# Cross-attention's output chain moved to other slots, context rounding split, weight loads of the feed-forward stage moved

## What is computed

```
x = layernorm(x + self_attention(x))         # LoRA linears, 16 heads of 32
x = layernorm(x + cross_attention(x, ctx))   # 16 heads of 16 channels
x = layernorm(x + ffn(x))                    # fp8 rounding, gelu gate, hidden 2048
```

## Time and profile before

| | us |
|---|---|
| median of 3 runs | 1977.44 |
| lowest and highest | 1976.67, 1979.93 |
| profiled execution, its own time | 1983.12 |
| its span, first to last instruction | 1981.2 |
| busy in the span: PE, DVE, ACT, POOL | 1900.6, 1495.3, 1124.2, 981.4 |
| mean granted TensorE clock | 0.972 |

### The profile page before, as it was taken

One profiled execution on the slowest core, in us unless ns is written; L12 is line 12 of the kernel. 1 busy time (PEld: TensorE's weight loads), 2 busy tenths in 40 slices (PEclk: granted clock), 3 DMA queues, 4 the chain that ended last, 5 costly groups with the idle time before them and its releaser, 6 DMA issues.

```text
span 1981.2 us, 31819 instructions
## 1 busy us (share of the span) xinstructions
PE 1900.6 (96%) x11460; PEld 1056.7 (53%) x11460; DVE 1495.3 (75%) x2632; ACT 1124.2 (57%) x2117; POOL 981.4 (50%) x968
## 2 busy tenths in 40 slices
PE   7999999999999898999999999999999899999997
PEld 4677777777777544444444444444444334444443
DVE  3566666666675667788888888888888439999997
ACT  3345444444444526888888888888887653333330
POOL 3455546555465423444444445445443237666664
PEclk9999999999999869999999999999999879999999
DMA  5665565655646521334443333334343300111111
GB/s 169 173 165 142 145 166 134 158 140 141 171 117 165 141 78 40 120 111 125 138 141 112 106 108 107 111 104 119 119 120 118 131 28 12 44 43 43 65 43 43
DMA packets 149899, 220.56 MB, mean 111 GB/s; under 512 B 41847, under 2 KB 50551, under 8 KB 148999
## 3 DMA queue, kind: packets, MB, share of 16 engines
q1 hardware_dynamic: 140078, 216.96, 38.0%
q10 hardware_dynamic: 9664, 1.58, 0.5%
HBM read 83.95 MB, written 32.02 MB: 59 GB/s over the span
## 4 chain that ended last, share of the span: by engine, by line
PE 65%; DVE 14%; DMA 7%; POOL 6%; issue 3%; SPq 2%; ACT 2%; ACTq 0%; DVEq 0%; POOLq 0%
PE bank L1287 9%; PE bank L1322 9%; PE bank L1616 8%; PE bank L85 7%; PE bank L86 6%; PE bank L87 6%; PE bank L1330 5%; PE bank L1592 5%; PE bank L577 4%; DMA xa_den<-inv 3%; PE bank L631 2%; DVE sa_mneg L703 2%; PE bank L644 2%; DVE sa_xnat L717 2%; DVE xa_mneg L1365 2%
## 5 line engine op out<-in xcount | busy, mean ns | idle before, releaser
L1365 DVE TENSOR_REDUCE xa_mneg<-bank 128x1 f32<-128x512 f32 x1024 | 643.7, 683 | 134.3 <-PE bank L1330 132.5
L1186 ACT ACTIVATE xa_prob<-bank 128x512 f32<-128x512 f32 x1024 | 549.0, 605 | 88.0 <-PE bank L1322 84.8
L1330 PE MATMUL bank<-xa_kst,xa_qst 48*128 48x512 f32 x1024 | 386.0, 462 | 14.5 <-DMA xa_kst<-xa_part_k 8.9
L1322 PE MATMUL bank<-xa_qst,xa_kst 49*128 49x512 f32 x1024 | 367.4, 447 | 15.5 <-ACT xa_prob L1186 15.2
L468 ACT ACTIVATE sa_prob<-bank 128x512 f32<-128x512 f32 x256 | 152.2, 598 | 333.7 <-PE bank L631 332.9
L1322 PEld LDWEIGHTS bank<-xa_qst,xa_kst 49*128 49x128 f32 x1024 | 167.5, 188 | 305.1 <-ACT xa_prob L1186 248.1
L1287 PE MATMUL bank<-xa_prob,xa_v 128*32 128x512 f32 x2048 | 280.0, 619 | 0.0
L1524 POOL TENSOR_TENSOR ff_total<-ff_prod,ff_mag 128x512 f32<-128x512 bf16 x128 | 194.3, 1518 | 96.7 <-DVE ff_mag L1640 96.7
L1330 PEld LDWEIGHTS bank<-xa_kst,xa_qst 48*128 48x128 f32 x1024 | 165.4, 188 | 55.5 <-DVE xa_mneg L1365 37.4
L703 DVE TENSOR_REDUCE sa_mneg<-bank 128x2 f32<-128x512 f32 x256 | 164.1, 682 | 35.1 <-PE bank L644 34.9
L1568 ACT ACTIVATE ff_gelu<-bank 128x512 bf16<-128x512 f32 x128 | 75.7, 593 | 156.7 <-PE bank L1616 156.7
(11 more groups left out here) (191 smaller groups left out, 3626.9 us busy)
## 6 DMA issues: line engine op xcount, KB each, us to landing
xa_qst<-xa_part_q SPq DMA_DIRECT2D x192, 128.0 KB, 3.5
xa_kst<-xa_part_k SPq DMA_DIRECT2D x192, 128.0 KB, 2.8
sa_qst<-sa_part_qh SPq DMA_DIRECT2D x64, 256.0 KB, 4.1
sa_kst<-sa_part_kh SPq DMA_DIRECT2D x64, 256.0 KB, 5.4
xa_den<-inv SPq DMA_DIRECT2D x64, 256.0 KB
sa_xraw<-xT SPq DMA_DIRECT2D x32, 256.0 KB, 4.3
sa_qst<-sa_part_ql SPq DMA_DIRECT2D x32, 256.0 KB, 4.0
sa_kst<-sa_part_kl SPq DMA_DIRECT2D x32, 256.0 KB, 5.8
```

Source lines behind the costliest of these rows:

```text
L1186: act.activation(prob[place[e]][:, :], banks[eb[e]][:, :], ACT.Exp, scale=X_SCALE)\
L1322: pe.matmul(banks[eb[e]][:, :], kst[u % 3][rows_of, head // 2, t * P:(t + 1) * P], qst[u % 3][rows_of, head // 2, :], start=True, stop=Tru ...
L1330: pe.matmul(banks[mb[m]][:, :], qst[u % 3][rows_of, n // 8, t * P:(t + 1) * P], kst[u % 3][rows_of, n // 8, :], start=True, stop=True).the ...
L1365: dve.tensor_reduce(mneg[:, u % 2, column:column + 1], banks[mb[m]][:, :], AX.X, ALU.max, negate=True).then_inc(s_mfree, 1)
```

## The change

- Output chain, first half: reciprocal at 5 (was 8), write of `inv` at 6 (was 9), spread read of `den` at 10 (was 13), product on POOL at 14 (was 17).
- Output chain, second half: reciprocal and write stay at 8 and 9; `den` at 12 (was 13), product at 16 (was 17). The sum of the halves at 33 (was 34).
- The context load moves from 64b-28 to 64b-27, which puts it behind the second half's `den` on SP.
- The rounding of x and context is two instructions each (one per half of the channels), at 64b-14 and -11 for x, and 64b and +5 for the context; the low parts follow one slot later each. Semaphore counts follow.
- `bn_stats` and `bn_aggr` move three slots behind the residual addition, the factor on POOL from 2 to 5 slots behind it.
- The feed-forward phase's first step moves from slot 1022 to 1032. The two x2 loads of its second step move to its fifth (slot 1086, was 1046).
- `down` waits for `hq` piece by piece and no longer for all 16 at once.

```
     LAST = BATCH * (NB + 1) + 40
+    HIGH_AT = {"x": (-14, -11), "c": (0, 5)}
...
     def output_half(slot, after):
-        halves, left = divmod(slot - OUT_AT - after, S // 2)
-        return divmod(halves, 2) if left == 0 and 0 <= halves < 2 * U else None
+        for half, slots in enumerate(after if isinstance(after, tuple) else (after, after)):
+            u, left = divmod(slot - OUT_AT - half * S // 2 - slots, S)
+            if left == 0 and 0 <= u < U:
+                return u, half
+        return None
...
-    def high_x(act, wait, b):
+    def high_x(act, wait, b, i):
...
-        act.activation(xh[:, :, :], x1[b % 4][:, :, :], ACT.Copy).then_inc(s_hi, 1)
+        act.activation(xh[:, i, :], x1[b % 4][:, i, :], ACT.Copy).then_inc(s_hi, 1)
...
-            if (un := output_half(slot, 9)):
+            if (un := output_half(slot, (6, 9))):
...
-            if (un := output_half(slot, 13)):
+            if (un := output_half(slot, (10, 12))):
...
-            if (b := batch(slot, -28)):
+            if (b := batch(slot, -27)):
                 load_c(sp, wait, b)
...
-            if (un := output_half(slot, 17)):
+            if (un := output_half(slot, (14, 16))):
...
-            if (un := unit(slot, OUT_AT + 34, 1)):
+            if (un := unit(slot, OUT_AT + 33, 1)):
...
-            if (b := batch(slot, -13)):
-                low_x(pool, wait, b)
-            if (b := batch(slot, 1)):
-                low_c(pool, wait, b)
-            for job in jobs_in.get(slot - 2, []):
+            for i in range(CC):
+                if (b := batch(slot, HIGH_AT["x"][i] + 1)):
+                    low_x(pool, wait, b, i)
+                if (b := batch(slot, HIGH_AT["c"][i] + 1)):
+                    low_c(pool, wait, b, i)
+            for job in jobs_in.get(slot - 5, []):
...
-                    wait.wait_ge(s_pjfree, n + 1)
-                    dve.bn_stats(stats[:, t, :], x[:, t, :]).then_inc(s_bn, 1)
+            for job in jobs_in.get(slot - 3, []):
+                if job[0] == "o":
+                    _, b, t = job
+                    wait.wait_ge(s_pjfree, at[job] + 1)
+                    dve.bn_stats(stats[:, t, :], x1[b % 4][:, t, :]).then_inc(s_bn, 1)
...
-            if (un := output_half(slot, 8)):
+            if (un := output_half(slot, (5, 8))):
...
-        yield
+        for _ in range(4):
+            yield
         left.stacks(wait, 2)
         load(1)
         load(2)
-        for _ in range(PRELUDE - 2 + 2 * HT):
+        for _ in range(PRELUDE - 5 + 2 * HT):
             yield
...
             n = 4 * p + t
             wait.wait_ge(s_wo, 16)
-            wait.wait_ge(s_hq, HT * (p + 1))
             wait.wait_ge(s_sum, n - 1)
...
             for h in range(HT):
+                wait.wait_ge(s_hq, HT * p + h + 1)
                 last = pe.matmul(lb[n % 2][:, :], hq[p % 2][:, h, t * P:(t + 1) * P],
                                  wo[:, h, :], start=(h == 0), stop=(h == HT - 1))
...
-FFN_AT = [1022, 1046, 1070, 1078, 1086, 1094, 1108]
+FFN_AT = [1032, 1046, 1070, 1078, 1086, 1094, 1108]
```

More of the change, by code:

```diff
@@ L960, in load_c @@
     def load_c(sp, wait, b):
-        wait.wait_ge(s_hi, 2 * b)
-        wait.wait_ge(s_low, 2 * b)
+        wait.wait_ge(s_hi, 4 * b)
+        wait.wait_ge(s_low, 4 * b)
         sp.dma_start(craw[:, :, :], rows(a["c"], b)).then_inc(s_c, 16)
-    def high_x(act, wait, b):
+    def high_x(act, wait, b, i):
         wait.wait_ge(s_x1[b % 4], 16 * (b // 4 + 1))
@@ L968, in high_x, with high_c @@
             wait.wait_ge(s_pj, at["q", 2 * b - 1] + 1)
-        act.activation(xh[:, :, :], x1[b % 4][:, :, :], ACT.Copy).then_inc(s_hi, 1)
-    def high_c(act, wait, b):
+        act.activation(xh[:, i, :], x1[b % 4][:, i, :], ACT.Copy).then_inc(s_hi, 1)
+    def high_c(act, wait, b, i):
         wait.wait_ge(s_c, 16 * (b + 1))
@@ L974, in high_c, with low_x, low_c @@
             wait.wait_ge(s_pj, at["v", b - 1, 1] + 1)
[L975 to L979, removed]
+        act.activation(ch[:, i, :], craw[:, i, :], ACT.Copy).then_inc(s_hi, 1)
+    def low_x(engine, wait, b, i):
+        wait.wait_ge(s_hi, 4 * b + i + 1)
+        engine.tensor_tensor(xl[:, i, :], x1[b % 4][:, i, :], xh[:, i, :].bitcast(F32),
                              ALU.subtract).then_inc(s_low, 1)
-    def low_c(engine, wait, b):
-        wait.wait_ge(s_hi, 2 * b + 2)
-        engine.tensor_tensor(cl[:, :, :], craw[:, :, :], ch[:, :, :].bitcast(F32),
+    def low_c(engine, wait, b, i):
+        wait.wait_ge(s_hi, 4 * b + 2 + i + 1)
+        engine.tensor_tensor(cl[:, i, :], craw[:, i, :], ch[:, i, :].bitcast(F32),
                              ALU.subtract).then_inc(s_low, 1)
@@ L1089, in gpsimd @@
         yield
-        low_x(pool, wait, 0)
+        for i in range(CC):
+            low_x(pool, wait, 0, i)
         yield
-        low_c(pool, wait, 0)
+        for i in range(CC):
+            low_c(pool, wait, 0, i)
         yield
@@ L1157, in scalar @@
         yield
-        high_x(act, wait, 0)
+        for i in range(CC):
+            high_x(act, wait, 0, i)
         high_w("k")
         yield
-        high_c(act, wait, 0)
+        for i in range(CC):
+            high_c(act, wait, 0, i)
         high_w("v")
@@ L1232, in scalar @@
                        .then_inc(s_y, 1)
[L1233 to L1236, removed]
+            for i in range(CC):
+                if (b := batch(slot, HIGH_AT["x"][i])):
+                    high_x(act, wait, b, i)
+                if (b := batch(slot, HIGH_AT["c"][i])):
+                    high_c(act, wait, b, i)
     def tensor(pe):
@@ L1259, in project_part @@
             else:
-                wait.wait_ge(s_hi, 2 * b + (1 if name == "q" else 2))
-                wait.wait_ge(s_low, 2 * b + (1 if name == "q" else 2))
+                wait.wait_ge(s_hi, 4 * b + (2 if name == "q" else 4))
+                wait.wait_ge(s_low, 4 * b + (2 if name == "q" else 4))
             if i == 0:
```

## The result

The changed kernel takes 1946.47 us (median of 4 runs, 1945.07 to 1948.51), the kernel before beside it 1978.68 (4 runs). The ratio is 0.9833 [0.9809, 0.9857], some 33 us less.

A forecast was written before the change was run, and what follows sets the result against it. PE was taken as the bound, gaining only where it idles or runs at half clock. Terms 3.5 (output chain) + 2.0 (weight loads) + 5.1 (end) = 10.6 us, from 1977.44 to 1966.8 us; range 1956.0 to 1974.0.

The forecast's parts named there:

- The bound of 7.1 us: Steady part, 850 to 1500 us: PE busy 642.9 of 650 us at full clock, so only 7.1 us open to gain.
- Split rounding, later statistics: Steady part: split rounding adds 0.16 us per tensor on ACT, POOL's factor is in time; zero, feed-forward order up to 1 us.
- Output chain: Steady part: second half's den lands some 2.2 us sooner, gain 3.5 us, between 0 and 5; first half gains nothing.
- rival 2: Only the end gains: den stays at 5.9 us, the stall moves from stacks to DVE; 1972.3 us, chance 0.16.
- rival 4: Slower: reciprocal at slot 5 blocks DVE in every batch, PE runs out of banks; 1985.3 us at 1.0 us, chance 0.03.
- Weight loads: Slot 1032: PE's 8.91 us wait goes, a DVE wait of some 6 us comes; net gain 2 us, from -2 to 13.
- rival 1: Sums slip past the weight loads or loads run faster, no stall at 1535 us; about 13 us, 1955.8 us, chance 0.18.
- half clock paid again: Behind the new gap at the weight loads, ten slots again take 10.5 us where full clock needs about 6.5: 4 us.
- rival 3: Clock stays full in the 29 us from 1587; some 8 us more gained, 1958.8 us, chance 0.08.
- x2 loads: Slot 1086: they hold unit 30's last inv by 6.3 us at most, against 8.1 us of cover; zero.
- The end: Last four groups of `down`: PE starts on `hq` pieces without the 4.62 us wait; gain 5.1 us, 3.4 with half clock.
- common offset: Whole kernel: the median lies 5.7 us below the profiled execution, carried over unchanged to the forecast.

## Why the prediction was wrong, point by point

**The bound of 7.1 us.** The prediction's "PE is busy 642.9 of 650 us at full clock, so 7.1 us are open there" is the failed step. The steady gain was read from PE's idle time alone, 3.5 us for 12 batches; some 23 us were gained. The waits of before, 900 to 1480 us, had a hint. The same view, before first, then after (engine, tile and line, what it waited for: us in total, times, longest):

```profile
PEld bank L1322 <- ACT xa_prob L1186: 158.5, 195, 2.1
...
PEld bank L1330 <- DVE xa_mneg L1365: 21.0, 66, 0.4
```
```profile
PEld bank L1333 <- ACT xa_prob L1196: 159.1, 195, 1.9
...
PEld bank L1341 <- DVE xa_mneg L1376: 12.5, 46, 0.3
```

PE's weight loads (PEld) waited 66 times, 21.0 us in all, for a bank that DVE still had; in the changed kernel 46 times, 12.5 us. Such waits leave PE busy: in the timelines below matmuls recorded with 0.50 us start 0.34 us apart, so a delay of 0.16 us between two of them shows no idle time. The view does not price the waits, though. Its largest row, for the exponentials, is the same in both kernels, and the chain's part of the gain is not in it (23.9 us for DVE in 850 to 1500 us with the chain alone, as before). The Trainium skill's page "Perfetto Trace Analysis", section "Identifying the Most-Contended Engine", warns of just this: matmul busy share is not a good measure of what is left, and the busy share of weight loads is one of two that it names instead. The trace agrees: PE's busy share was 98.9% (642.86 of 650) with some 20 us open, while that of PEld was 45.4% (294.89) and rose to 46.9% (304.72). The prediction should have weighed that rule.

**"Split rounding, later statistics: all zero."** Right for the rounding, wrong for the statistics: 1.19 us in each batch, 14 us over twelve. The prediction asked only whether ACT gets its factor in time; that DVE does the statistics in front of the maxima that PE waits for was not in it. The timeline of DVE just after an o projection, kernel before:

```profile
1362.16 0.75 DVE L1386 SCALAR_TENSOR_TENSOR xa_x<-bank,xa_bo,xa_x 128x512 f32<-128x512 f32 x1 [1.15 <-PE bank L87]
1362.94 0.69 DVE L1389 BATCH_NORM_STATS2 xa_stats<-xa_x 128x6 f32<-128x512 f32 x1
1363.67 0.18 DVE L1392 BATCH_NORM_AGGREGATE xa_mv<-xa_stats 128x2 f32<-128x6 f32 x1
1363.77 3.65 DVE L1365 TENSOR_REDUCE xa_mneg<-bank 128x1 f32<-128x512 f32 x6
```

PE's projection of six matmuls keeps DVE idle for 1.15 us; then DVE owes the residual, the statistics and the maxima of the slots that follow. Its next six reductions run without a break, 0.61 us each, and PE's MAX matmuls come at exactly that pace, though each slot's reduction was meant to hide behind 0.83 us:

```profile
1364.48 0.49 PE L1330 MATMUL bank<-xa_kst,xa_qst 48*128 48x512 f32 x1
...
1365.08 0.49 PE L1330 MATMUL bank<-xa_kst,xa_qst 48*128 48x512 f32 x1
...
1365.68 0.49 PE L1330 MATMUL bank<-xa_kst,xa_qst 48*128 48x512 f32 x1
```

In the changed kernel the debt is smaller by 0.9 us, and at the same place the MAX matmuls follow each other after 0.34 and 0.47 us. The statistics come three reductions later. DVE then works without a break up to the next product that is not for it, the value projection, which leaves it idle for 0.89 us:

```profile
1346.42 0.50 PE L1341 MATMUL bank<-xa_kst,xa_qst 48*128 48x512 f32 x1
...
1346.76 0.40 PE L1341 MATMUL bank<-xa_kst,xa_qst 48*128 48x512 f32 x1
...
1347.23 0.50 PE L1341 MATMUL bank<-xa_kst,xa_qst 48*128 48x512 f32 x1
```
```profile
1344.63 0.75 DVE L1397 SCALAR_TENSOR_TENSOR xa_x<-bank,xa_bo,xa_x 128x512 f32<-128x512 f32 x1 [0.50 <-PE bank L87]
1345.30 1.88 DVE L1376 TENSOR_REDUCE xa_mneg<-bank 128x1 f32<-128x512 f32 x3
1347.09 0.68 DVE L1403 BATCH_NORM_STATS2 xa_stats<-xa_x 128x6 f32<-128x512 f32 x1
...
1351.85 0.69 DVE L1376 TENSOR_REDUCE xa_mneg<-bank 128x1 f32<-128x512 f32 x1 [0.89 <-PE bank L1341]
```

On average, DVE's step from one maximum to the next at the two projections of a batch fell from 2.87 to 1.92 and from 3.30 to 1.85 us, and rose by 0.82 where the statistics now stand. With the statistics alone they are 2.05 and 2.25 us, so a part of the second is the chain's. "DVE is busy 544 of 650 us" was an average that said nothing of this place.

**Output chain.** Mechanism right (`den` ahead of the loads, 4.0 us and not 5.8, waits for `ol` gone, rival 2 out), size too small: 0.70 us a batch, 8.4 over twelve, against 3.5. The idle time read was only its visible half. The first half's earlier reciprocal costs nothing in the steady part; rival 4 did not occur.

**Weight loads.** Sums late, DVE 7.38 us at the reciprocal, PE's gap 6.12 us: as forecast, and rival 1 did not occur. Of the 6.4 us gained in 864 to 960, about 2 belong to the statistics (alone: 89.2 to 87.4) and 0.8 to the chain (alone: 88.4), so some 3.5 and not 2 to the loads. The mis-sized term is the half clock paid again. Before, it lasted from 1536.7 for 17.1 us, 9.8 us beyond the gap; after, from 1521.8 for 6.8 us, 3.9 us beyond. That length is not fixed by the gap: behind gaps of 6.1 to 6.2 us it was 3.9, 4.8 and 6.8 us in three kernels.

**Exponential 960 to 1023.** This is rival 3, which had a chance of 0.08: the half clock that lasted 27.3 us from 1587.9 lasts 6.8 us from 1559.4, and 7.4 us are gained, of 8 estimated. It is not firmly the change's own. With `down` alone, whose edit acts later, this stretch takes 53.6 us, with the rounding alone 50.6, with the statistics one slot on 48.3 and with the chain alone 49.9, against 57.2; the full change without the statistics has 53.8. The 57.2 are the longest of all kernels that have the weight loads where before or after has them, and the profiled execution of before lies 5.7 us above its median, that of after only 2.0 above its own. So a part of these 7.4 us is the one execution that was profiled. Why the clock rose sooner stays open, and "the work reaches it in another rhythm" is not shown: just before it fell, PE was busy for about 90% of the time in both (8.97 of 10 us before 1588, 4.52 of 5 us before 1559), and in it nearly without a gap in both. The single executions of the kernel before scatter over 1970 to 1987 us too, the longer the lower their mean clock (1987.16 at 0.970, 1970.15 at 0.979).

**x2 loads.** Zero, as forecast: issued at 1558.85, they made `inv` and `den` late (6.6 us from issue to issue where 1.96 are usual), and the cover held.

**The end.** 4.9 us against 5.1, in the full change and alone. PE's two waits are 1.01 and 0.21 us, and the added waits cost nothing.

**What was missing.** The wait of ACT for the factor of the last batch, +6.8 us. "POOL is now ready after 5" was checked against ACT's slot 11 of the steady part, and the last batch has another distance, 6. With it found and the statistics priced at 14 us, the sum would have been 3.5 + 14 + 2 + 5.1 - 6.8 = 17.8 us. The rest is the chain's hidden half (5), the clock behind exponential 960 (7), and 1 to 2 at the weight loads: some 31 us, where the medians differ by 32 and the profiled executions by 34.5. The "common offset" of 5.7 us was not common. Of the prediction's sums one is a slip without weight: the chances for "faster" add up to 0.89 and not 0.88.

## What to carry to other kernels

A PE that is busy for 99% of a stretch may still wait: divide busy time by matmuls, look at what its weight loads wait for, and compare equal batches with each other, before taking the idle share as the bound on a gain. Work of an engine that PE depends on through a few banks should not stand right behind a product that kept that engine idle; three to six slots later it cost less here. When a step is moved by slots, check the distance to its reader in every region, the last units included, and send bulk loads in single pieces where no small transfer of the critical chain follows at once.

## What the runs showed that I had not expected

- PE's busy time held some 20 us in 650 that the same work did without in the changed kernel, seen as 164.7 against 159.7 ns per matmul.
- With the chain changed, eight equal batches take the same time to within 0.08 us; before, they differ by up to 1.65 us. Each of the four steady batches that had 3.4 us of half clock in it (two with the statistics alone, one with the rounding alone, one with the statistics one slot on) took at least 1.3 us longer than the batches beside it.
- Behind 4 MB, 8 KB landed 10.5 us after their issue, and the 8 KB of `inv` held SP for 11.5 us in another placing, so that POOL waited 13.92 us for `den`; the same bytes sent in pieces left PE without a gap.
- A longer half clock follows one gap than another: 9.8 us beyond a gap of 8.91, 3.9 beyond one of 6.12, 6.8 beyond one of 6.24, 5.2 beyond one of 3.39. It is not in proportion to the gap.
